# First two expert-tile steps placed in the drain of the second pass, table pieces and bias products placed elsewhere

## The chip, the cores and the metric

The kernel runs on one core of one Trainium2 chip. The metric is the device time of one execution in microseconds (us), lower is better. The engines are TensorE (PE in the rows; PEld is its weight load), VectorE (DVE), ScalarE (ACT), GpSimd (POOL) and SyncE (SP), which only issues DMAs. Every engine runs its own instruction list in order and waits on semaphores.

## What is computed

Two layers over x (16 sequences x 128 tokens x 128) and a context (16 x 120 x 128), float32:

```python
x = x + L0_xattn(layernorm(x), ctx, ctx)     # 16 heads of 8, temperature per head from score statistics
x = x + L0_ffn(layernorm(x))                 # RMS norm, router, top 2 of 8 experts, up 128->512, u * silu(gate), down 256->128
x = x + L1_xattn(layernorm(x), ctx, ctx)     # 8 heads of 128, windows of 64 keys with dilation 1, 2, 4, 8, biases bq, bk, bv, bc
x = x + L1_ffn(layernorm(x))                 # router with softmax, top 2 of 8 experts, gelu, 128->64->128
```

## The kernel before, in words

The work goes in stages. A first pass over the 16 sequences computes the scores and their statistics, then the weights are turned or multiplied on TensorE. The **second pass** (software pipeline with the `b_` functions) computes the first attention, its residual, the norm, the router's logits and the top two experts of each sequence. Then come the **tiles** of the first feed-forward layer (`ct_` functions), the **second attention** (`c_` and `d_` functions, with the norm of each sequence as its `c` tail), and the second feed-forward layer (`e_` functions).

*The second pass.* `software_pipeline` writes out one step after the other. A stage with lag k handles sequence `step - k` in that step. Sixteen sequences with lags up to 7 give 32 steps, 0 to 31, the ones from 16 on being the **drain**. On TensorE the stages of one step are, in this order: logits of sequence step-6, scores of step-1, the turn (transpose) of the normed rows of step-5, the projection of step-3, the output of step-2, and then the parts with a step number, `b_rank` and `attention_biases`. VectorE has at the end of its step the highest logits of sequence step-6 and `b_route`, which picks experts of a batch of four sequences (`pick_experts`, steps 9, 13, 17, 21), places its rows (`place_rows`, one step later, after TensorE's `rank`) and computes pieces of the tile tables (`tile_table`). GpSimd has the norm's power function (`tail_rstd`) of sequence step-3 and two scatters per step from step 11 on (`scatter`, 32 in all): each writes 128 normed rows to their places in the DRAM tensor `by_expert`, which is sorted by expert.

*The tiles.* The 4096 rows (2048 tokens, two experts each) are handled as 39 tiles of 128 rows in three phases: 9 tiles need batches 0 and 1 (scatters 0 to 15), 8 more need batch 2, and the last 22 need batch 3. Which expert a tile has and where its rows lie are data: `tile_table(k, piece)` computes the table of phase k on one partition of VectorE, in five pieces, and SyncE, ScalarE and TensorE read it into registers (`read_four`, line 457, waits for the semaphore `k_tab`). SyncE loads a tile once its table and its scatters are there (`load_tile`, wait for `k_tab` at line 465, for the scatters at 578, the DMA at 581), six tiles ahead in a ring of four, and stores the result (585). `tile_pipeline` (line 685) writes out the steps: in step n TensorE turns tile n (`ct_turn`, its matmul is line 1649), multiplies tile n-1 by the expert's up weights (`ct_up_project`, 1870) and tile n-2 by its down weights (`ct_down_project`, 1881). ScalarE copies the up weights of tile n (`ct_weights`, 826), computes the gate of tile n-1 (831) and copies the result of tile n-2 (837). VectorE copies the turned tile n (`ct_turned`, 1502), forms the product of tile n-1 (`ct_product`, 1508), and then does `ct_route`: in step 0 the copy of the bias sum, in steps 1 to 5 the pieces of table 2.

*The start of the second attention.* TensorE computes the keys of two pairs of sequences, then for sequences 0 and 1 the values, the turn of the normed rows (`c_turn`), and the scores, and then a software pipeline. VectorE combines the two expert rows of a sequence (`c_combine`, lines 1514 and 1518, inside `d_combine`), takes its statistics (1257, 1267), applies the norm (`c_norm`, 1280), and does parts of the softmax (`d_scores`, `d_weights`). GpSimd gathers the two expert rows of each sequence with two indirect DMAs (`gather`, 1065), and computes the norm's factor (`tail_rstd`, 990 and 992). `d_add_bias` (1084) adds the bias row to x.

*The bias products.* `attention_biases` (line 1746) sums bc and, over eight heads, the product of the value bias with Wc into one PSUM place: one product with `ones` and eight with a broadcast column of `bqk1`, each two matmul records in the trace. VectorE copies the sum into `bias_rows`.

## Time and profile before

| | us |
|---|---|
| median of 3 runs | 423.95 (422.66 to 426.68) |
| profiled execution, its own time | 422.5 |
| its span | 420.6 |
| busy in the span: TensorE, its weight load | 358.2 (85%), 277.4 (66%) |
| VectorE, ScalarE, GpSimd | 310.2 (74%), 279.4 (66%), 200.1 (48%) |
| mean granted TensorE clock | 0.935 of full speed |

The span is 1.9 us shorter than the execution's own time; what lies around it is launch and end. The busy time of an engine is an average over stages. The page cuts the span into 40 slices of 10.5 us and gives each engine one digit per slice (9 is 90% or more), and one for the clock that TensorE was granted:

```profile
PE   1776796655979999997699999978999999969996
PEld 0432342223766676666599999847888888756886
DVE  3599999998445999899664444378988988886752
ACT  1399999998565566642277887647888788673330
POOL 2554445554001443887779000278887783532200
PEclk9989869985889999998599999999999999997999
```

The second pass lies in slices 12 to 19 (from 120 us), the tiles in 19 to 25, the second attention in 25 to 36. The slices 18 and 19 (189 to 210 us) and 25 to 27 (263 to 294 us) hold the two borders that the change touches.

### The profile page before, as it was taken

What the parts mean: (1) busy time and instruction counts of PE and PEld (TensorE: products, weight loads), DVE (VectorE), ACT (ScalarE), POOL (GpSimd) and SP (SyncE); (2) the same over time, 40 slices, a digit from 0 to 9 for tenths busy, and PEclk for the clock granted to TensorE, in tenths of its full rate; (3) what the DMA queues carried; (4) which work ended last, traced back from release to release, by engine and by line L of the source; (5) the groups of instructions that cost most, each with busy time, mean ns of one, the idle gap of its engine ahead of it and who ended that gap; (6) DMA issues with size and microseconds to landing.
All of it is one profiled execution on the core that took longest, in us unless ns stands there. A gap on an engine that the chain in (4) does not pass through costs nothing.

```text
span 420.6 us, 12481 instructions
## 1 busy us (share of the span) xinstructions
PE 358.2 (85%) x4117; PEld 277.4 (66%) x4117; DVE 310.2 (74%) x1149; ACT 279.4 (66%) x844; POOL 200.1 (48%) x357
## 2 busy tenths in 40 slices
PE   1776796655979999997699999978999999969996
PEld 0432342223766676666599999847888888756886
DVE  3599999998445999899664444378988988886752
ACT  1399999998565566642277887647888788673330
POOL 2554445554001443887779000278887783532200
PEclk9989869985889999998599999999999999997999
DMA  5999799500010000011243332111110010000011
GB/s 109 108 302 314 199 289 291 127 2 0 2 40 6 3 6 5 29 35 34 88 124 106 95 89 83 39 39 40 27 30 25 19 27 4 2 2 1 10 43 50
DMA packets 58497, 29.88 MB, mean 71 GB/s; under 512 B 15810, under 2 KB 56004, under 8 KB 58436
## 3 DMA queue, kind: packets, MB, share of 16 engines
q1 hardware_dynamic: 53652, 23.83, 21.8%
q0 software_dynamic: 2048, 4.20, 3.5%
q10 hardware_dynamic: 2736, 1.07, 1.2%
q8 instruction: 34, 0.56, 0.6%
q14 instruction: 27, 0.22, 0.2%
HBM read 13.82 MB, written 15.27 MB: 69 GB/s over the span
## 4 chain that ended last, share of the span: by engine, by line
PE 47%; DVE 20%; issue 11%; ACT 9%; POOL 6%; DMA 2%; ACTq 2%; SPq 1%; POOLq 0%; DVEq 0%
PE psum L1870 9%; PE psum L1649 6%; ACT wa L739 5%; PE psum L1881 4%; PE psum L1895 4%; PE psum L1684 3%; DVE scored L1165 3%; DVE negmax L1152 2%; DVE work L1233 2%; PE psum L1918 2%; POOL rstd L986 2%; PE psum L2008 2%; ACTq L697 2%; PE psum L1934 2%; PE psum L1952 2%
## 5 line engine op out<-in xcount | busy, mean ns | idle before, releaser
L739 ACT ACTIVATE wa<-psum,negmax 128x120 f32<-128x120 f32 x256 | 68.3, 440 | 2.0 <-DVE negmax L1152 1.9
L1065 POOL DMA_INDIRECT c_area<-by_expert,rows_at x32 | 31.4, 980 | 50.4 <-DMA by_expert<-c_area 38.8
L1684 PE MATMUL psum<-wa 64*128 64x480 f32 x128 | 41.8, 738 | 9.6 <-issue 7.5
L954 POOL TENSOR_TENSOR wa<-kT,cst 128x960 f32<-128x960 f32 x16 | 28.6, 1791 | 37.9 <-ACT kT L720 35.0
L1165 DVE BATCH_NORM_STATS2 scored<-wa 128x6 f32<-128x240 f32 x128 | 43.2, 400 | 4.2 <-issue 4.2
L771 ACT ACTIVATE work<-psum 120x1024 f32<-120x1024 f32 x32 | 31.0, 1022 | 19.6 <-PE psum L1806 19.6
L1870 PE MATMUL psum<-c_area,work 128*128 128x128 f32 x312 | 42.8, 282 | 0.1
L1870 PEld LDWEIGHTS psum<-c_area,work 128*128 128x128 f32 x312 | 39.2, 197 | 0.3 <-issue 0.3
L1508 DVE TENSOR_TENSOR c_area<-psum,c_area 128x256 f32<-128x256 f32 x39 | 16.6, 425 | 30.8 <-ACT c_area L831 27.4
L1152 DVE TENSOR_REDUCE negmax<-psum 128x8 f32<-128x960 f32 x32 | 36.7, 1146 | 2.7 <-PE psum L1684 2.4
L1025 POOL DMA_INDIRECT by_expert<-scored,rows_at x32 | 32.2, 1006 | 8.9 <-issue 8.3
L1895 PE MATMUL psum<-ctxS,qk 128*128 128x256 f32 x128 | 29.8, 379 | 0.0
L1649 PE MATMUL psum<-cst,work 128*128 128x128 f32 x120 | 21.7, 329 | 6.3 <-issue 4.2
L852 ACT ACTIVATE work<-work,d 128x128 f32<-128x128 f32 (+1 forms) x64 | 23.1, 371 | 5.2 <-DVE d L1543 5.2
L826 ACT COPY work<-upT 128x512 f32 x39 | 24.1, 621 | 2.9 <-issue 2.9
L846 ACT COPY work<-psum 128x1024 f32<-128x1024 f32 x16 | 16.2, 1011 | 14.0 <-PE psum L1918 13.9
L1895 PEld LDWEIGHTS psum<-ctxS,qk 128*128 128x128 f32 x128 | 23.6, 193 | 2.6
L1649 PEld LDWEIGHTS psum<-cst,work 128*128 128x128 f32 x120 | 16.8, 170 | 11.8 <-issue 8.8
L1881 PE MATMUL psum<-dnT,c_area 128*128 x156 | 23.9, 276 | 0.6 <-DVE c_area L1508 0.6
L1684 PEld LDWEIGHTS psum<-wa 64*128 64x128 f32 x128 | 12.4, 222 | 17.6 <-issue 17.5
L1671 PEld LDWEIGHTS psum<-wa,w4T 128*128 128x128 f32 x32 | 5.4, 213 | 28.0 <-ACT wa L727 28.0
L881 ACT ACTIVATE work<-psum,uvec 128x256 f32<-128x256 f32 x56 | 22.0, 472 | 2.7 <-PE psum L1895 2.7
(275 smaller groups left out, 988.8 us busy)
## 6 DMA issues: line engine op xcount, KB each, us to landing
by_expert<-work SPq DMA_DIRECT2D x12, 768.0 KB, 6.6
c_area<-by_expert SPq DMA_DIRECT2D x39, 64.0 KB, 1.9
by_expert<-c_area SPq DMA_DIRECT2D x39, 64.0 KB, 1.6
x<-in_x_dram ACTq DMA_DIRECT2D x16, 64.0 KB, 3.7
work<-in_L_ffn_w_down_dram SPq DMA_DIRECT2D x1, 1024.0 KB
wa<-mscratch SPq DMA_DIRECT2D x64, 2.0 KB
out_dram<-wa SPq DMA_DIRECT2D x32, 32.0 KB, 1.6
wa<-in_ctx_dram SPq DMA_DIRECT2D x16, 60.0 KB, 3.6
```

The lines of the kernel that those rows point to most:

```text
L739: e = nc.scalar.activation(prob[:, z, head, :], psum[:, score_bank(b, half) + h // 4, (h % 4) * LK:(h % 4 + 1) * LK], ACT.Exp, bias=negmax ...
L771: nc.scalar.activation(probT[:, z, half * HALF0:(half + 1) * HALF0, :].rearrange("p h q -> p (h q)"), psum[0:LK, 2 * half:2 * half + 2, :] ...
L954: nc.gpsimd.tensor_tensor(kexp[:, z], kT[:, b, :].unsqueeze(1).to_broadcast([P, HALF0, LK]), halfscale.unsqueeze(2).to_broadcast([P, HALF0 ...
L1025: nc.gpsimd.indirect_dma_start(by_expert[:, :], bass.IndirectOffsetOnAxis(rows_at[:, i:i + 1], 0), xrow[:, BATCH * r + i % BATCH, :], None ...
L1065: nc.gpsimd.indirect_dma_start(y_rows[:, r, j, :], None, by_expert[:, :], bass.IndirectOffsetOnAxis(rows_at[:, i:i + 1], 0)).then_inc(ld_y ...
L1152: nc.vector.tensor_reduce(negmax[:, z, :].rearrange("p (a c h) -> p a c h", a=2, c=2)[:, :, half], banks(score_bank(b, half), 2)[:, :, 0:4 ...
L1165: s = nc.vector.bn_stats(bnout[:, bass.ds(b * HALF0 + h // 2, 1), :].rearrange("p a s -> p (a s)"), prob[:, z, h:h + 2, :].rearrange("p h ...
L1649: return nc.tensor.transpose(dst, src, ident[0:k, 0:k])
L1684: m = nc.tensor.matmul(psum[:, score_bank(b, half) + g, 0:4 * LK], qs[rows, z, :], kexp[rows, z, 4 * half:4 * half + 4].rearrange("p i k - ...
L1870: m = nc.tensor.matmul(psum[:, n % 2, j * P:(j + 1) * P], ct_w[:, n % 2, j * P:(j + 1) * P], ct_xT[:, n % 2, :], start=True, stop=True)
L1881: m = nc.tensor.matmul(psum[:, 4, 0:D], ct_h[:, n % 2, j * P:(j + 1) * P], w, start=(j == 0), stop=(j == DN_TILES - 1))
L1895: m = nc.tensor.matmul(psum[:, bank + i // 2, 2 * P * (i % 2):2 * P * (i % 2 + 1)], qk1[:, 4 * half + i, :], ctxS[:, 2 * p:2 * p + 2, :].r ...
```

## The change

It has four parts. (1) The pieces of table 0, in steps 15 to 18 of the second pass, are placed in steps 15 to 17. (2) Steps 0 and 1 of the tile pipeline are placed at the end of steps 20 and 21 of the second pass, on TensorE, ScalarE and VectorE (`SEAM`, `seam_tiles`; `rest_tiles` writes the remaining steps). (3) The pieces of table 1, in steps 19 to 21 of the second pass, are placed in tile steps 0 to 4, and those of table 2 in tile steps 5 to 9, not 1 to 5. (4) The bias products, in steps 18 and 19 of the second pass, are placed around the first turns of the second attention; VectorE copies their sum there, behind the norm of sequence 1 and ahead of combining sequence 2. Their place in PSUM and that of three small buffers change with it.

```diff
...
@@ -668,8 +668,9 @@
         RAMP, EARLY_PAIRS = 2, 2
         PICK_AT = {BATCH * (r + 1) - 1 + LOGITS_B: r for r in range(BATCHES)}
         TABLE_PIECES = 5
-        PIECES_AT = {15: ((0, 0),), 16: ((0, 1), (0, 2)), 17: ((0, 3),), 18: ((0, 4),),
-                     19: ((1, 0), (1, 1)), 20: ((1, 2), (1, 3)), 21: ((1, 4),)}
+        PIECES_AT = {15: ((0, 0), (0, 1)), 16: ((0, 2), (0, 3)), 17: ((0, 4),)}
+        SEAM = {NB + 4: 0, NB + 5: 1}
+        TABLE_AT = {**{n: (1, n) for n in range(TABLE_PIECES)}, **{n + TABLE_PIECES: (2, n) for n in range(TABLE_PIECES)}}
         SCATTERS = {BATCH + LOGITS_B + 1 + i: range(2 * i, 2 * i + 2) for i in range((BATCHES - 1) * BATCH)}
 
         def after(first, stage):
@@ -684,10 +685,19 @@
 
         def tile_pipeline(stages, lag=5):
 
-            for n in range(TILES + lag):
+            def step(n):
                 for late, stage in stages:
                     if 0 <= n - late < TILES or late == 0:
                         stage(n - late)
+
+            def seam(b, z):
+                if b + 7 in SEAM:
+                    step(SEAM[b + 7])
+
+            def rest():
+                for n in range(len(SEAM), TILES + lag):
+                    step(n)
+            return seam, rest
 
 
         @block.scalar
@@ -813,9 +823,6 @@
                     nc.scalar.activation(nat0[:, 3, 0:1], eps[:, 1:2], ACT.Silu)
 
             act.wait_ge(wt_dve, copied_by_dve(C_GROUPS - 1))
-            software_pipeline(act, [(6, b_logits), (1, b_softmax(0)), (1, b_softmax(1)), (5, tail_evict("b")),
-                                    (7, lambda b, z: b_halves(b + 7))], peel=NB)
-
             staged = {}
 
             def ct_weights(n):
@@ -836,7 +843,10 @@
                     act.wait_ge(st_ct[n % RING_C], 16 * (n // RING_C))
                 nc.scalar.copy(ct_y[:, n % RING_C, :], psum[:, 4, 0:D]).then_inc(ct_ye, 1)
 
-            tile_pipeline([(0, lambda n: ct_weights(n) if n < TILES else None), (1, ct_gate), (2, ct_result)], lag=2)
+            seam_tiles, rest_tiles = tile_pipeline([(0, lambda n: ct_weights(n) if n < TILES else None), (1, ct_gate), (2, ct_result)], lag=2)
+            software_pipeline(act, [(LOGITS_B, b_logits), (1, b_softmax(0)), (1, b_softmax(1)), (5, tail_evict("b")),
+                                    (7, lambda b, z: b_halves(b + 7)), (7, seam_tiles)], peel=NB)
+            rest_tiles()
 
 
             def d_vw_copy(b, z):
@@ -1418,11 +1428,6 @@
                 for piece in PIECES_AT.get(step, ()):
                     tile_table(*piece)
 
-            software_pipeline(dve, [(0, b_expand), (3, b_residual), (3, tail_stats("b", b_x1)), (4, tail_norm("b")),
-                                    (4, tail_rms), (2, b_add_bias), (2, b_recip),
-                                    (3, tail_aggr("b")), (2, b_norm), (0, b_constants), (LOGITS_B, b_highest),
-                                    (7, lambda b, z: b_route(b + 7))], peel=NB)
-
             r_done, r_after = counted(r_dve)
 
             def route_logits(half):
@@ -1487,11 +1492,8 @@
                                         own[:, at, :].unsqueeze(2).to_broadcast([P, SEQS, LQ]), ALU.mult).then_inc(e_gm, 1)
 
             def ct_route(n):
-                if n == 0:
-                    dve.wait_ge(l1_pe, L1_SUMS)
-                    nc.vector.tensor_copy(bias_rows[:, 0, :], psum[:, 5, 384:384 + D]).then_inc(l1_dve, 1)
-                elif n - 1 in range(TABLE_PIECES):
-                    tile_table(len(PHASES) - 1, n - 1)
+                if n in TABLE_AT:
+                    tile_table(*TABLE_AT[n])
                 elif n == TILES - 4:
                     expert_weights()
 
@@ -1524,7 +1526,12 @@
                 for stage in (c_combine, c_stats, c_aggr):
                     stage(b, z)
 
-            tile_pipeline([(0, lambda n: ct_turned(n) if n < TILES else None), (1, ct_product), (0, ct_route)], lag=1)
+            seam_tiles, rest_tiles = tile_pipeline([(0, lambda n: ct_turned(n) if n < TILES else None), (1, ct_product), (0, ct_route)], lag=1)
+            software_pipeline(dve, [(0, b_expand), (3, b_residual), (3, tail_stats("b", b_x1)), (4, tail_norm("b")),
+                                    (4, tail_rms), (2, b_add_bias), (2, b_recip),
+                                    (3, tail_aggr("b")), (2, b_norm), (0, b_constants), (LOGITS_B, b_highest),
+                                    (7, lambda b, z: b_route(b + 7)), (7, seam_tiles)], peel=NB)
+            rest_tiles()
 
 
             def d_keys(p, half):
@@ -1614,6 +1621,8 @@
             d_combine(1, 1)
             d_scores(0, 0)
             c_norm(1, 1)
+            dve.wait_ge(l1_pe, L1_SUMS)
+            nc.vector.tensor_copy(bias_rows[:, 0, :], psum[:, BANK_TAIL, 384:384 + D]).then_inc(l1_dve, 1)
             d_combine(2, 0)
             d_weights(0, 0)
             c_norm(2, 0)
@@ -1743,18 +1752,17 @@
             weights(range(10, N_GROUPS))
 
 
-            def attention_biases(step):
-
-                dst = psum[:, 5, 384:384 + D]
-                if step == NB + 2:
-                    pe.wait_ge(b_x1, NB)
+            def attention_biases(heads):
+
+                dst = psum[:, BANK_TAIL, 384:384 + D]
+                if heads.start == 0:
                     pe.wait_ge(l1_dve, 2)
+                    pe.wait_ge(b_lk, NB)
                     nc.tensor.matmul(dst, ones[0:1, :], bc1[:, :], start=True, stop=False)
-                heads = {NB + 2: range(3), NB + 3: range(3, H1)}.get(step, ())
                 for h in heads:
                     m = nc.tensor.matmul(dst, bqk1[:, 2, h:h + 1].to_broadcast([P, P]), wcT[:, h, :],
                                          start=False, stop=(h == H1 - 1))
-                if step == NB + 3:
+                if heads.stop == H1:
                     m.then_inc(l1_pe, 1)
 
             def tail_turn(ph):
@@ -1768,7 +1776,6 @@
                         if ph == "b":
                             pe.wait_ge(b_lk, b)
                     if ph == "c" and b == 0:
-                        pe.wait_ge(l1_dve, L1_DONE)
                         pe.wait_ge(k_rows, BATCHES)
                     if ph == "d":
                         pe.wait_ge(tails["c"]["ev"], min(NB, b + TAIL_D + RAMP - TURN_C))
@@ -1850,9 +1857,6 @@
                 if step - 1 in PICK_AT:
                     rank(PICK_AT[step - 1])
 
-            software_pipeline(pe, [(LOGITS_B, tail_logits("b", routerT)), (1, b_scores), (5, tail_turn("b")),
-                                   (3, b_project), (2, b_output), (7, lambda b, z: b_rank(b + 7)),
-                                   (7, lambda b, z: attention_biases(b + 7))], peel=NB)
             tile_expert = {}
 
             def ct_turn(n):
@@ -1882,7 +1886,10 @@
                                          start=(j == 0), stop=(j == DN_TILES - 1))
                 m.then_inc(ct_dn, 1)
 
-            tile_pipeline([(0, lambda n: ct_turn(n) if n < TILES else None), (1, ct_up_project), (2, ct_down_project)], lag=2)
+            seam_tiles, rest_tiles = tile_pipeline([(0, lambda n: ct_turn(n) if n < TILES else None), (1, ct_up_project), (2, ct_down_project)], lag=2)
+            software_pipeline(pe, [(LOGITS_B, tail_logits("b", routerT)), (1, b_scores), (5, tail_turn("b")),
+                                   (3, b_project), (2, b_output), (7, lambda b, z: b_rank(b + 7)), (7, seam_tiles)], peel=NB)
+            rest_tiles()
 
 
             def d_keys(p, half):
@@ -1946,8 +1953,7 @@
             def d_output_whole(b, z):
                 pe.wait_ge(d_aT, b + 1)
                 pe.wait_ge(d_vw, b + 1)
-                if b:
-                    pe.wait_ge(d_x, b)
+                pe.wait_ge(*((d_x, b) if b else (l1_dve, L1_DONE)))
                 for h in range(2):
                     nc.tensor.matmul(d_sum, a1T[:, z, h * P:(h + 1) * P], vw[:, (b + 1) % RING_V, h * D:(h + 1) * D], start=(h == 0), stop=False)
 
@@ -2039,7 +2045,10 @@
             for b in range(2):
                 d_values_whole(b, b)
                 d_values_tiles(b, b)
+                if b == 0:
+                    attention_biases(range(0, 3))
                 c_turn(b, b)
+                attention_biases((range(3, 5), range(5, H1))[b])
                 d_scores_whole(b, b)
                 d_scores_tiles(b, b)
             software_pipeline(pe, [(RAMP + TURN_D, d_turn), (RAMP + TAIL_D, tail_turn("d")), (RAMP + LOGITS_D, tail_logits("d", router1)),
```

## Rows read from the trace of the kernel before

**Rows 1.** chain of waits, 195 to 212: start us, length us, engine, tile, line, count
```profile
196.48 1.58 PE psum L1755 x6
...
199.07 2.13 PE psum L1755 x10
...
202.68 0.61 PE psum L1791 x2
...
204.46 0.62 DVE work L1322
```

**Rows 2.** waits of SyncE's queue, 150 to 300: total us, times, longest
```profile
SPq L465 <- DVE tile_tab L1389: 21.7, 1, 21.7
...
SPq L578 <- DMA by_expert<-scored,rows_at: 3.1, 1, 3.1
```

**Rows 3.** GpSimd in time order: start, length, line, operation, [idle before <- releaser]
```profile
197.62 0.21 POOL L980 TENSOR_TENSOR rstd<-mv,both 128x2 f32<-128x2 f32 x1
...
200.46 0.96 POOL L1025 DMA_INDIRECT by_expert<-scored,rows_at  x1 [0.30 <-issue]
```

**Rows 4.** DMA issues: tensors, queue, count, KB each, median us to landing
```profile
c_area<-by_expert SPq DMA_DIRECT2D x39, 64.0 KB, 1.9
...
by_expert<-scored,rows_at POOLq DMA_INDIRECT x32, 2.3
```

**Rows 5.** SyncE in time order: first loads of the tiles
```profile
202.91 7.04 SPq L581 DMA_DIRECT2D c_area<-by_expert  x7
```

**Rows 6.** TensorE in time order, first tile steps
```profile
205.82 0.48 PE L1649 MATMUL psum<-cst,c_area 128*128 128x128 f32 x1
...
207.31 1.93 PE L1870 MATMUL psum<-c_area,work 128*128 128x128 f32 x8
209.03 0.42 PE L1649 MATMUL psum<-cst,c_area 128*128 128x128 f32 x1
...
212.53 0.27 PE L1649 MATMUL psum<-cst,c_area 128*128 128x128 f32 x1
212.64 1.06 PE L1870 MATMUL psum<-c_area,work 128*128 128x128 f32 x8
...
213.98 0.27 PE L1649 MATMUL psum<-cst,c_area 128*128 128x128 f32 x1
...
215.76 0.30 PE L1649 MATMUL psum<-cst,c_area 128*128 128x128 f32 x1
```

**Rows 7.** windows: length; TensorE, weight loads, VectorE, ScalarE, GpSimd busy; granted clock; DMA
```profile
194.00:198.00 4.00, 3.05 (x23) 2.60 (x23) 3.68 (x23) 0.00 (x0) 3.30 (x6) 0.80 0.08 26
...
206.00:210.00 4.00, 3.23 (x15) 2.96 (x16) 1.65 (x9) 0.72 (x2) 3.09 (x4) 0.50 0.29 90
210.00:214.00 4.00, 4.00 (x37) 3.98 (x36) 2.83 (x13) 2.80 (x8) 3.09 (x4) 1.00 0.35 105
```

**Rows 8.** VectorE in time order, end of the second pass
```profile
197.11 0.18 DVE L1267 BATCH_NORM_AGGREGATE mv<-bn 128x2 f32<-128x6 f32 x1
...
198.17 0.15 DVE L1381 TENSOR_SCALAR tile_tab<-small 1x9 uint32<-1x9 f32 x1
...
199.24 0.33 DVE L1280 TENSOR_SCALAR xn<-x,mv,rstd 128x128 f32<-128x128 f32 x1
```

**Rows 9.** TensorE in time order, start of the second attention
```profile
276.65 0.33 PE L1649 MATMUL psum<-cst,c_area 128*128 128x128 f32 x1 [0.79 <-DVE c_area L1280]
...
281.04 0.33 PE L1649 MATMUL psum<-cst,c_area 128*128 128x128 f32 x1 [0.17 <-DVE c_area L1280]
...
291.20 0.66 PE L1649 MATMUL psum<-cst,work 128*128 128x128 f32 x4 [1.29 <-DVE work L1557]
```

**Rows 10.** VectorE in time order, start of the second attention
```profile
280.93 0.36 DVE L1514 SCALAR_TENSOR_TENSOR x<-c_area,ew_t,x 128x128 f32<-128x128 f32 x1
...
289.36 0.48 DVE L1280 TENSOR_SCALAR c_area<-x,work 128x128 f32<-128x128 f32 x1 [0.85 <-POOL work L992]
```

**Rows 11.** GpSimd in time order, start of the second attention
```profile
282.32 0.19 POOL L990 TENSOR_TENSOR work<-work,eps 128x1 f32<-128x1 f32 x1 [0.39 <-DVE work L1267]
```

More of the change, by code:

```diff
@@ L372, in build @@
         total_ps = keep[0:1, 192:192 + NE]
-        in_c = (area(13184, 12).rearrange("p (z s) -> p z s", z=2), area(13196, 4).rearrange("p (z s) -> p z s", z=2),
-                area(13200, 8).rearrange("p (z s) -> p z s", z=2),
+        in_c = (area(W_C, 12).rearrange("p (z s) -> p z s", z=2), area(W_C + 12, 4).rearrange("p (z s) -> p z s", z=2),
+                area(W_C + 16, 8).rearrange("p (z s) -> p z s", z=2),
                 c_area[:, 3840:4096].rearrange("p (z d) -> p z d", z=2), None)
```

## The prediction

> **What bounds the kernel now.** I read the page's slices first: TensorE is nearly full in the tiles and in the second attention, so a change at the two borders between stages pays only as far as those full stretches start earlier. Then the chain of waits over the first border. In [rows 1] the bias products of TensorE (six, then ten matmuls at the lower clock) stand on the chain, and behind them the last sequence's router logits at 202.68 and its picks on VectorE, done at 204.46 + 0.62 = 205.08. So the products do delay the last picks. But the first tile needs something else too, and for that I read the waits of SyncE's queue [rows 2]: it waited 21.7 us for the first table and then, with the table there, another 3.1 us for rows that GpSimd scatters. The table was not last. GpSimd computes the last sequence's norm at 197.62 without any idle time before it, and issues the sixteenth scatter, the last one that tile 0 needs, at 200.46 [rows 3]; this lands 2.3 us later [rows 4], at 202.8, and the first load is issued at 202.91 [rows 5]. With 1.9 us to landing [rows 4] tile 0 is there at 204.8. TensorE turns it at 205.82 [rows 6], after ranking the last batch.
>
> **Part 1: the first table one step earlier.** It was not awaited last, so nothing is won. What does it cost? VectorE is busy 3.68 of 4 us before the border [rows 7]: it is the engine that sets the pace there. Its last piece ran from 198.17 to 199.24, behind the statistics of the last sequence at 197.11 [rows 8]. Now all five pieces stand ahead of these statistics: 199.24 - 198.17 = 1.07 us later, done at 197.11 + 0.18 + 1.07 = 198.36. GpSimd, which started on them at 197.62, starts at about 198.4 instead: its sixteenth scatter, tile 0's load and its landing all come 0.8 us later, at L = 205.6. Bounds: 0 (if VectorE's gaps take the pieces) and 1.1 us. I take 0.8, since 3.68 of 4 us leaves no gap for it.
>
> **Part 2: two tile steps in the drain.** On TensorE the turn of tile 0 now stands ahead of the last sequence's logits, and it waits for the load until L. Before, the logits ran at 202.68. Queued behind the wait are the logits, then the picks on VectorE, the ranks and the last batch's row places. From L: turn and copy to SBUF as before; the logits slip in beside that copy; the second turn at L + 0.8; the up products of tile 0 at L + 1.0, 1.93 us at the lower clock [rows 6], until L + 2.8 as TensorE issues. The picks take, from logits to end, 205.08 - 202.68 = 2.4 us [rows 1], and VectorE has a table piece of about 0.6 us in front of them: they end at about L + 2.9, after the up products. Then the rank, 205.82 - 205.08 = 0.7 us [rows 1, 6], and the turn of tile 2 at L + 3.7 = 209.3. Before it was at 209.03 [rows 6]. So the first border gives nothing: +0.3 us. The two steps are inside the drain by their place in the program, but they run at the time at which they ran before, since the data arrives then. Bounds: with L at 204.8, and the rank hidden behind the up products, -1.3 us; with one more tile step at the lower clock, +1.7 us. I take +0.3, which the rows give directly.
>
> What leaves this stretch is the bias work: 18 matmuls. The copy of the sum by VectorE also leaves; it was beside other work. ScalarE's copies of the weights and its first gate are small and find the engine idle. SyncE's order of loads and stores is the same; tile 9's load now waits for a table that ends with tile step 4, about when the load's ring is free anyway (its turn comes four steps later).
>
> **Part 3: both later tables among the tiles.** A tile step is 1.45 us (213.98 - 212.53), and one in which VectorE has a long table piece was 215.76 - 213.98 = 1.78 us, 0.33 more [rows 6]. Before, five pieces lay in tile steps; now ten do, two of them in the drain. The new ones are of eight tiles, not 22, hence shorter; only the last, with its bookkeeping for the next table, is as long. One such loss and a bit: +0.4 us, bounds 0 and 3 x 0.33 = 1.0.
>
> **Part 4: the bias products in the second attention.** At the higher clock eight matmuls start over 1.06 - 0.27 us, 0.11 each [rows 6]. The first group (8 matmuls, 0.9 us) stands before the turn at 276.65, where TensorE idled 0.79 [rows 9]: 0.1 us at most. The second (4, 0.4 us) runs while ScalarE copies that turn. The third (6 matmuls) follows the turn at 281.04 [rows 9]; TensorE itself would wait there for ScalarE, so on TensorE it is hidden. But VectorE now waits for the sum, in order, right before it combines sequence 2. Queued behind this wait: that combination (before at 280.93, without idle time) [rows 10], its statistics, the first softmax weights. The sum is there at 281.15 + 6 x 0.11 + 0.27 = 282.1; with the copy VectorE goes on at 282.3. That is 1.3 us late. Is that hidden? GpSimd waited 0.39 us for exactly these statistics at 282.32 [rows 11], and from there it is full: gathers of sequences 4 and 5, the norm of sequence 3, for which VectorE waits 0.85 us at 289.36 [rows 10], and with that TensorE at 291.20 (1.29 us idle) [rows 9], where its full stretch begins. Each link is the late one, so the 1.3 us go through. Bounds: 0 (if the sum is ready before VectorE comes to it) and 1.8 us (six matmuls at 0.21 each, the pace of the lower clock).
>
> **Sum.** 0.3 + 0.4 + 1.3 = +2.0 us, on the profiled execution's 422.5 us: 424.5. The three timed runs have a median of 423.95 and spread over 4 us, so the profiled one is at the low end; the four values together have a middle of 423.3. I predict the median as 423.3 + 2.0 = 425.3 us.
>
> **Rivals.**
> (A) *The freed TensorE wins.* VectorE's earlier pieces fall into gaps, tile 0 lands at 204.8 as before, its up products start near 205.9, not 207.31, and the wait at the second attention is hidden: -1.4 + 0.4 + 0 = -1.0, 422.3 by the middle above. For: the products are on the chain [rows 1]. Against: VectorE has no gaps [rows 7], and GpSimd sets the load.
> (B) *TensorE's clock stays low longer; slower.* The granted clock was 0.50 (1.2 GHz) from 206 to 210, and 1.00 (2.4 GHz) in the next 4 us [rows 7], after some 3 us of dense products that followed a sparse stretch. Now TensorE has no bias products and waits about 4 us for tile 0, then alternates with VectorE. If the rise comes later, each tile step at the lower clock has 12 matmuls and a turn at 0.21 instead of 0.11 us, about 1.35 us more. It decides from two steps on: 2.0 + 2.7 = +4.7, 428.0. Against: from L on the density is nearly what it was from 205.8 on.
> The Trainium skill (TensorE: Matmul & The Clock Gate, "What's actually happening") says the same as a rule: the throttled state is the default, and sustained activity releases it. By that rule, thinning out TensorE's work ahead of the tiles speaks against this change.
> (C) *Only the second border is harmless:* the sum is awaited in time that VectorE would lose anyway. +0.7, 424.0. Against: VectorE showed no idle time at 280.93.
>
> **How the numbers follow.** Forecast 0.55, A 0.14, B 0.12, C 0.14, something unseen 0.05. 1% of this kernel, 4.2 us, is what a measurement can tell from no change. The forecast, A and C lie within it. Slower by over 1%: most of B, and a little of the forecast with the spread of the runs: 0.14. Faster by over 1%: a slice of A and of the unseen, 0.07. The range: 421.5 (A with its spread) to 428.6 (B, and the upper bounds of parts 2 and 4); its own width for the forecast alone is 423.3 to 427.2.
>
> **What would show it.** SyncE's wait for the scattered rows longer than 3.1 us, and the wait for the table shorter by the same reordering; the first load issued near 203.7; the last logits right behind the turn of tile 0, near 206, instead of 202.68; the turn of tile 2 within 0.5 us of 209.03; one or two tile steps above 1.45 us more than before; VectorE idle about 1 us before the copy of the bias sum, released by TensorE; the first idle-free turn of the attention 2 us after 291.20. The prediction is wrong if the load of tile 0 is issued before 203, if tile 2 is turned before 208, or if GpSimd does not wait longer for the statistics of sequence 2.

## The result and the profile after

The changed kernel takes 428.39 us (median of 8 runs, 425.57 to 430.48), the kernel before beside it 423.47 us (8 runs, 422.46 to 426.68): a ratio of 1.0087, 95% interval 1.0051 to 1.0123. Run a second time it took 428.23 us against 424.01 (medians of 12 and 29 runs), ratio 1.0078 (1.0036 to 1.0120). Each ratio is an estimate over the runs and not the quotient of the two medians, which lie 4.9 and 4.2 us apart here; it leaves out runs in a slower state, over 1.5% above the fastest of their kernel (one each of e2_late_copy and e7_bias_late, three of e12_all_three). So the changed kernel is slower by 0.8 to 0.9%, some 3.5 us, by the ratios, and by 1.0 to 1.2% by the medians; the forecast was 425.3 us, +2.0. Its lowest time is 3.25 us above the lowest of the kernel before in that second comparison (425.10 against 421.85), its highest 2.80 us (430.64 against 427.84): the whole spread has moved by about 3 us.

I call the first profiled execution of the changed kernel "after" (429.23 us, span 427.3) and the second one "the second profile" (425.76 us, span 423.9). They are 3.4 us apart, with one program; that is used below.

**The first border.** SyncE's queue in the changed kernel, 150 to 300 us: total wait, times, longest; it answers to [rows 2].

```profile
SPq L465 <- DVE tile_tab L1399: 20.0, 2, 19.5
...
SPq L578 <- DMA by_expert<-scored,rows_at: 6.5, 1, 6.5
```

The wait for the table is 2.2 us shorter than before (19.5 against 21.7), the wait for the scattered rows 3.4 longer (6.5 against 3.1): the earlier table buys nothing. GpSimd in time order (start, length, line, operation, idle before and its releaser), to be set beside [rows 3]:

```profile
199.16 0.19 POOL L990 TENSOR_TENSOR rstd<-mv,both 128x2 f32<-128x2 f32 x1 [0.63 <-DVE mv L1277]
...
202.02 0.96 POOL L1035 DMA_INDIRECT by_expert<-scored,rows_at  x1 [0.30 <-issue]
```

The last norm had no idle time before it; now GpSimd waits 0.63 us for VectorE's statistics, which stand behind the table. The sixteenth scatter is at 202.02, not 200.46, and the first load at 204.48, not 202.91. TensorE in time order, beside [rows 1, 6]:

```profile
206.48 0.48 PE L1658 MATMUL psum<-cst,c_area 128*128 128x128 f32 x1 [4.89 <-DMA c_area<-by_expert]
206.75 0.44 PE L1798 MATMUL psum<-routerT,xnT 128*128 128x8 f32 x2
207.44 0.45 PE L1658 MATMUL psum<-cst,c_area 128*128 128x128 f32 x1 [0.25 <-DVE c_area L1504]
207.67 1.94 PE L1874 MATMUL psum<-c_area,work 128*128 128x128 f32 x8
...
210.11 0.48 PE L1658 MATMUL psum<-cst,c_area 128*128 128x128 f32 x1
210.38 1.92 PE L1874 MATMUL psum<-c_area,work 128*128 128x128 f32 x8
212.09 1.06 PE L1885 MATMUL psum<-dnT,c_area 128*128 x4
212.94 0.42 PE L1658 MATMUL psum<-cst,c_area 128*128 128x128 f32 x1
```

TensorE stands 4.89 us before the turn of tile 0, and the last logits, at 202.68 before, are now behind it at 206.75. Tile 0's up products start at 207.67, 0.36 us later than before. Then comes what the sum did not hold: the second up products take 1.92 us, not 1.44, and the down products 1.06, not 0.61. The next two rows are windows (busy times of the five units, granted clock, DMA share and GB/s), first of "after", then of the second profile; they answer to [rows 7].

```profile
210.00:214.00 4.00, 4.00 (x21) 3.97 (x21) 2.52 (x13) 1.71 (x5) 3.09 (x4) 0.51 0.22 68
```

```profile
210.00:214.00 4.00, 4.00 (x36) 4.00 (x36) 2.96 (x16) 2.20 (x6) 2.97 (x4) 0.98 0.33 98
```

Before, the granted clock was 1.00 (2.4 GHz) in this window. In "after" it stayed at 1.2 GHz nearly to its end, in the second profile it did not. From 206 to 210 TensorE had been busy 3.27 of 4 us in "after", 3.75 in the second profile and 3.23 in the kernel before, where the clock rose early too; so the busy time in that window does not tell the two cases apart.

**The tables.** VectorE and then GpSimd in "after":

```profile
225.56 1.97 DVE L1399 TENSOR_SCALAR tile_tab<-small 1x22 uint32<-1x22 f32 x1
227.45 0.27 DVE L1504 COPY c_area<-psum 128x128 f32<-128x128 f32 x1
```

```profile
226.24 1.26 POOL L1050 TENSOR_TENSOR w_lo<-ew,w_hi 128x512 fp32r<-128x512 f32 x1
```

A write of 22 numbers takes 1.97 us, ends at 227.53, 0.03 us after GpSimd's subtraction (227.50), and TensorE waits 1.67 us for the copy behind it; this tile step is 3.37 us long, and 1.76 before. In the second profile the same write lies earlier:

```profile
223.72 0.17 DVE L1399 TENSOR_SCALAR tile_tab<-small 1x22 uint32<-1x22 f32 x1
...
225.94 0.42 DVE L1510 TENSOR_TENSOR c_area<-psum,c_area 128x256 f32<-128x256 f32 x1 [0.95 <-ACT c_area L838]
```

**The second border.** VectorE, GpSimd and TensorE in "after", to be set beside [rows 9, 10, 11]:

```profile
286.89 0.29 DVE L1625 COPY small<-psum 128x128 f32<-128x128 f32 x1 [1.09 <-PE psum L1763]
287.10 0.34 DVE L1516 SCALAR_TENSOR_TENSOR x<-c_area,ew_t,x 128x128 f32<-128x128 f32 x1
```

```profile
288.47 0.19 POOL L1000 TENSOR_TENSOR work<-work,eps 128x1 f32<-128x1 f32 x1 [2.06 <-DVE work L1277]
```

```profile
297.39 0.66 PE L1658 MATMUL psum<-cst,work 128*128 128x128 f32 x4 [1.56 <-DVE work L1564]
```

VectorE waits 1.09 us for the sum of the bias products and then copies it; GpSimd's wait grows from 0.39 to 2.06 us, and the turn at which the full stretch begins goes from 291.20 to 297.39.

**The loss by stretch.** Five points can be read in every trace: the first reciprocal of the second pass on VectorE (129.42 before), the turns of tile 4 (212.53) and tile 20 (236.44), the turn of [rows 9] at 291.20, and the end of the span (420.6). The stretches between them, each less that of the kernel before, in us:

| profiled execution | start | border 1 | tables | border 2 | rest | span |
|---|---|---|---|---|---|---|
| after | +0.44 | +1.87 | +2.25 | +1.63 | +0.51 | +6.7 |
| the second profile | -0.05 | +0.36 | +0.61 | +2.10 | +0.28 | +3.3 |
| e1_bias_in_drain | +3.95 | +1.26 | +0.64 | +0.01 | -0.06 | +5.8 |
| e2_late_copy | +0.12 | +1.88 | +2.26 | +0.22 | +0.52 | +5.0 |
| e3_no_seam | +0.10 | -0.19 | +0.81 | +1.61 | +0.57 | +2.9 |
| e4_bias_only | +0.82 | +0.68 | -0.14 | +2.17 | +0.57 | +4.1 |
| e10_pool_waits | -0.32 | +0.30 | +0.61 | +2.46 | +0.05 | +3.1 |
| e11_fill | +4.25 | +3.01 | +2.32 | +1.63 | +0.49 | +11.7 |
| e12_all_three | +0.45 | +2.69 | +0.40 | +0.23 | +0.43 | +4.2 |

Three things in it belong to no kernel but to the execution. (1) The start is near 0 or near +4 (+0.82 in e4). Windows of the kernel before and of e11_fill, 127 to 134 us, in code that no kernel here changes:

```profile
127.00:134.00 7.00, 6.76 (x158) 4.62 (x154) 3.36 (x8) 3.88 (x4) 0.59 (x2) 1.00 0.02 5
```

```profile
127.00:134.00 7.00, 6.47 (x80) 4.21 (x84) 0.33 (x1) 2.32 (x3) 0.30 (x1) 0.53 0.02 4
```

The same 7 us hold half the matmul records at half the clock (1.2 GHz); e1_bias_in_drain shows 0.51 there, e4 0.76. (2) At the first border the granted clock falls between 195.6 and 197.6 in each trace with a start near 0 (in e12 it is low once more before that, from 190.8 to 194.2), and is back near 210 (before, the second profile, e3, e10) or between 212.7 and 214.7 (after, e2, e4, e12). (3) The table write meets GpSimd's subtraction in after, e2 and e11, and in none with the early clock. So a comparison of two profiles needs partners of the same kind. The second profile is such a partner of the profile before, and its +3.3 us is what the ratios of the timed runs show too.

### The profile page after: what moved, and what is told of

Its sections match the earlier page's. It is cut to its first block, busy times and chain, and to the rows that moved or that the text cites. A ratio compares the mean times of both kernels' runs of the same rounds, so it can differ in the third digit from the quotient of the medians.

```text
span 427.3 us, 12481 instructions
## 1 busy us (share of the span) xinstructions
PE 358.6 (84%) x4117; PEld 277.6 (65%) x4117; DVE 311.7 (73%) x1149; ACT 279.5 (65%) x844; POOL 200.1 (47%) x357
## 3 DMA queue, kind: packets, MB, share of 16 engines
q10 hardware_dynamic: 2736, 1.07, 1.2%
## 4 chain that ended last, share of the span: by engine, by line
PE 47%; DVE 20%; issue 11%; ACT 9%; POOL 6%; DMA 2%; ACTq 2%; SPq 1%; POOLq 0%; DVEq 0%
PE psum L1874 8%; PE psum L1658 6%; PE psum L1902 6%; ACT wa L749 5%; PE psum L1885 4%; PE psum L1693 3%; DVE scored L1175 3%; PE psum L1925 2%; DVE negmax L1162 2%; DVE work L1243 2%; POOL rstd L996 2%; ACTq L707 2%; PE psum L2014 2%; PE psum L1941 2%; PE psum L1958 1%
## 5 line engine op out<-in xcount | busy, mean ns | idle before, releaser
L1874 PE MATMUL psum<-c_area,work 128*128 128x128 f32 x312 | 43.7, 285 | 0.0
L1874 PEld LDWEIGHTS psum<-c_area,work 128*128 128x128 f32 x312 | 40.1, 201 | 0.0
L1658 PE MATMUL psum<-cst,work 128*128 128x128 f32 x120 | 21.7, 329 | 7.8 <-issue 4.2
```

Source lines behind the costliest of these rows:

```text
L1658: return nc.tensor.transpose(dst, src, ident[0:k, 0:k])
L1874: m = nc.tensor.matmul(psum[:, n % 2, j * P:(j + 1) * P], ct_w[:, n % 2, j * P:(j + 1) * P], ct_xT[:, n % 2, :], start=True, stop=True)
```

## The experiments

The comparison of the first four was with 35 runs of the kernel before, median 424.24 us, that of the next four with 29 runs, median 424.01 us.

**e1_bias_in_drain**: part 4 undone, the rest of the change kept.

```diff
-                if b == 0:
-                    attention_biases(range(0, 3))
                 c_turn(b, b)
-                attention_biases((range(3, 5), range(5, H1))[b])
...
+                (7, lambda b, z: attention_biases({NB + 2: range(3), NB + 3: range(3, H1)}[b + 7])
+                    if b + 7 in (NB + 2, NB + 3) else None),
...
```

> The changed kernel with part 4 undone: the bias products stand again in steps 18 and 19 of the second pass, VectorE copies their sum in tile step 2. Theory (costs are: scatters later 0.7 us, TensorE's clock low longer 1.2, table pieces among tiles 0.5, bias sum awaited by VectorE in the second attention 1.6): the products run in time in which TensorE idles anyway before tile 0 arrives, so the turn of tile 0 stays near 206.5 and the 1.6 us at the second attention go: about 1.6 us below the changed kernel, ratio to before about 1.006; GpSimd's wait for the statistics of sequence 2 is 0.4 us again. Rival (the bias products cost the drain as much as they cost the attention): same time as the changed kernel, ratio 1.010, and the turn of tile 0 comes later than 206.5.

425.80 us, ratio 1.0036 (1.0002 to 1.0071). The second border costs +0.01 instead of +1.63 and +2.10: that loss is part 4's alone. More than half of the timed loss is gone with it (1.0087 and 1.0078 to 1.0036, though the intervals still touch).

**e2_late_copy**: as changed, but VectorE copies the sum behind the combination and the statistics of sequence 2.

```diff
             c_norm(1, 1)
-            dve.wait_ge(l1_pe, L1_SUMS)
-            nc.vector.tensor_copy(bias_rows[:, 0, :], ...)
             d_combine(2, 0)
+            dve.wait_ge(l1_pe, L1_SUMS)
+            nc.vector.tensor_copy(bias_rows[:, 0, :], ...)
```

> The changed kernel with VectorE's wait for the bias sum and its copy moved behind the combination of sequence 2. Theory (VectorE's wait in order is what costs): VectorE idles under 0.2 us there, GpSimd gets the statistics of sequence 2 about 1.3 us earlier and the first idle-free turn of the attention comes 1.3 us earlier relative to the last tile; ratio to before about 1.006. Rival (the products on TensorE themselves, or the gathers, set that stretch): less than 0.4 us are won.

426.52 us, ratio 1.0044 (1.0006 to 1.0082). VectorE in time order:

```profile
285.40 0.35 DVE L1516 SCALAR_TENSOR_TENSOR x<-c_area,ew_t,x 128x128 f32<-128x128 f32 x1
...
286.61 0.27 DVE L1626 COPY small<-psum 128x128 f32<-128x128 f32 x1
```

The combination starts with no idle time, the copy with none either, 1.2 us later: by then the sum is there. The second border costs +0.22. The 18 matmuls on TensorE are thus nearly free, and the place of one wait in VectorE's order was the price. Border 1 and the tables repeat those of "after" within 0.01 us, the held write of 1.96 us with them (tile step 3.36 us).

**e3_no_seam**: as changed, but no tile step in the drain.

```diff
-        SEAM = {NB + 4: 0, NB + 5: 1}
+        SEAM = {}
```

> The changed kernel with part 2 undone: no tile step in the drain, tables and bias products as changed. Theory (the wait for tile 0 ahead of the last logits holds up picks, ranks and with them dense work on TensorE): the last logits run near 202, the turn of tile 2 comes 0.5 to 1 us earlier than in the changed kernel, the clock rises 1 to 4 us earlier, and the kernel is 1 to 2 us faster than the changed one, ratio to before about 1.006. Rival (the two steps in the drain do help): slower than the changed kernel by 0.5 us or more, ratio above 1.010.

427.10 us, ratio 1.0067 (1.0032 to 1.0102). TensorE in time order:

```profile
201.76 0.60 PE L1798 MATMUL psum<-routerT,xnT 128*128 128x8 f32 x2 [0.46 <-ACT xnT L807]
...
206.03 0.48 PE L1658 MATMUL psum<-cst,c_area 128*128 128x128 f32 x1 [1.05 <-DMA c_area<-by_expert]
```

Without the bias products the last logits start 0.92 us earlier than in [rows 1], and the last ranking too; but now the first tile's load, 1.3 us later than before because of part 1, is awaited last. The border gives 0.19 us back where the seam, in an execution with the same clock, costs 0.36. The timed interval overlaps that of the changed kernel, so the gain from leaving the seam out is read from the traces alone.

**e4_bias_only**: only part 4; tables and tile steps where they were.

> The kernel before with part 4 alone. Theory: the drain loses up to 0.9 us (the turn of tile 0 can come at 204.9, when its rows land, instead of 205.8), the second attention costs 1.6 us more: 0.7 to 1.6 us slower than before, ratio 1.002 to 1.004. Rival (freeing TensorE in the drain is worth the 4 us that the products took on the chain): faster than before, ratio 0.996 or less.

425.18 us, ratio 1.0029 (0.9992 to 1.0066). The second border costs +2.17, the tables nothing. Its first border costs 0.68 with the late clock: the window from 210 to 214 has 0.66. So the late clock also comes in a kernel without the seam.

**after_again**: the changed kernel.

> The changed kernel itself, beside the next three. If the lost time is the change's own and not one chip's: a ratio of 1.0087 again, within 0.0035, the granted clock 0.5 until after the up products of tile 1, and the last piece of table 2 at 1.97 us, not 0.17, behind an operation of GpSimd. If the long last piece was a late fetch of instructions that depends on the chip or on the run: it is 0.17 here.

428.23 us, ratio 1.0078 (1.0036 to 1.0120), as told above. The loss is there again. But against the expectation the profile shows the early clock and a write of 0.17 us: so a loss of some 3 us is there without them, and the late clock and the held write come on top in some executions.

**e10_pool_waits**: GpSimd's subtraction waits until the last table is written (the added wait stands behind GpSimd's power operation; the expectation speaks as if it stood ahead of it).

```diff
+            pool.wait_ge(k_tab, len(PHASES))
             pool.wait_ge(rounded, 2)
```

> The changed kernel, but GpSimd begins its powers of the expert weights only when the last table is written (one wait more on GpSimd). Theory, that VectorE's write of the last table entries is held until GpSimd's subtraction ends: the write takes 0.17 us, tile step 10 takes about 1.5 us, not 3.4, and the time is 1.7 us less than that of the changed kernel on this chip (ratio 0.9960 to it), unless GpSimd's later start is missed by the gathers. Rival, a late instruction fetch on VectorE: the write still takes about 2 us and the time does not move.

427.34 us, ratio 1.0067 (1.0026 to 1.0107), 0.9 us below the changed kernel, which these intervals do not tell from nothing. Its profile has the early clock, and there the write (223.38, 0.17 us) is far ahead of the subtraction (225.49) anyway; nothing was to be taken away, and this run doesn't decide. **e11_fill** tells more.

**e11_fill**: 18 turns of the unit matrix on TensorE in step 20, where it waits for tile 0.

```diff
+            def keep_clock(step):
+                for _ in range({NB + 4: 18}.get(step, 0)):
+                    turn(psum[:, 3, 0:P], ident, P)
...
+                                   (7, lambda b, z: keep_clock(b + 7)), (7, seam_tiles)], peel=NB)
```

> The changed kernel, with 18 turns of the unit matrix more on TensorE in step 20 of the second pass, where it waits for the first tile; their results are not read. Theory B, that the low clock of the first tile steps costs one to two steps' worth: the granted clock rises before the first up products, these take about 1.1 us, not 1.9, and the third tile is turned 1 to 2 us earlier relative to the first load; the time is 1 to 2 us less than the changed kernel's. Rival, that data and VectorE set these steps: the clock rises, and the third tile's turn stays within 0.4 us.

429.73 us, ratio 1.0123 (1.0060 to 1.0185): not faster, and the border costs +3.01. TensorE in time order, then two windows:

```profile
205.81 3.84 PE L1658 MATMUL psum<-cst 128*128 128x128 f32 x18
210.95 0.33 PE L1658 MATMUL psum<-cst,c_area 128*128 128x128 f32 x1 [1.30 <-DMA c_area<-by_expert]
...
211.89 1.27 PE L1878 MATMUL psum<-c_area,work 128*128 128x128 f32 x8
```

```profile
209.00:212.00 3.00, 1.36 (x10) 1.06 (x9) 0.65 (x3) 0.55 (x2) 2.39 (x3) 0.95 0.49 152
213.00:219.00 6.00, 5.44 (x34) 5.18 (x34) 3.27 (x16) 2.06 (x5) 4.58 (x5) 0.50 0.28 87
```

The clock did rise with the fillers, the first up products took 1.27 us, not 1.93. But TensorE then idled for the load, busy 1.36 of 3 us, and the clock was 0.50 again from 213 to 219, through the dense steps. Fillers that end before the work begins raised the clock here for the idle time. Of the +3.01 us, 1.74 lie ahead of the first load and 1.27 between it and the turn of tile 4, where "after" has 1.13 and 0.74. The third turn comes 5.5 us after the first load, as in the changed kernel (5.6 and 5.5 us): that is the rival's case. The profiled execution is the slowest of the six timed ones. The Trainium skill, "TensorE: Matmul & The Clock Gate", section "What's actually happening", ties the clock to TensorE's recent activity; both edges here agree in kind (the same fillers in e12, below, were followed by no rise), while the two profiles of the changed kernel, alike in activity and 3.7 us apart in the rise, show that this case's rows don't suffice to forecast the edge. The held write is in this trace on another line:

```profile
230.20 1.69 DVE L1391 TENSOR_SCALAR tile_tab<-small 1x22 uint32<-1x22 f32 x1
```

```profile
230.60 1.26 POOL L1050 TENSOR_TENSOR w_lo<-ew,w_hi 128x512 fp32r<-128x512 f32 x1
```

It ends at 231.89, again 0.03 us after the subtraction's 231.86. A late fetch of VectorE's code would belong to a place in its code; this stall goes with the subtraction. No run moved the subtraction away from a write that it would have met.

**e12_all_three**: the changed kernel with e2's late copy, e10's wait and e11's fillers.

> The changed kernel with all three: GpSimd's powers after the last table, the turns of the unit matrix in step 20, and the copy of the bias sum behind the combination of sequence 2. If the three terms add (1.7, 1 to 2, 1.3 us): 4 to 5 us less than the changed kernel, and so 0 to 1.5 us less than the kernel before, ratio 0.9965 to 1.0. If each is taken back by the next late one (the last picks, the gathers, the norm of sequence 3): 1 to 2 us less than the changed kernel, and still slower than the kernel before.

428.34 us, ratio 1.0065 (1.0015 to 1.0115): it is no better than the changed kernel by any bound that counts. The second border is cheap again (+0.22 in e2, +0.23 here): this term comes back. The write takes 0.17 us in spite of the late clock, but not by the added wait: the write ends at 226.51, GpSimd's power runs until 227.12, and the subtraction follows it (227.10) without idle time. The first border costs +2.69, with the rise only at 214.7. This time no rise followed the fillers; TensorE in time order, then a window in them and one behind them:

```profile
202.36 4.05 PE L1659 MATMUL psum<-cst 128*128 128x128 f32 x18
```

```profile
204.00:205.00 1.00, 1.00 (x7) 1.00 (x6) 0.00 (x0) 0.00 (x0) 0.74 (x1) 0.50 0.20 66
...
209.00:210.00 1.00, 1.00 (x6) 1.00 (x6) 0.93 (x5) 0.00 (x0) 0.70 (x2) 0.50 0.52 152
```

Nor is the +2.69 the fillers' cost. Tile 0's load is at 205.45, 0.97 us later than in "after"; GpSimd had waited 1.64 us for statistics until 195.73 (0.62 in "after"), right behind the stretch from 190.8 to 194.2 in which the granted clock was low, and well ahead of the fillers. From the turn of tile 0 to that of tile 4 it is 8.35 us, as in "after" (8.36). One of the three terms comes back, the other two were not put to the test that they were meant for.

**On one other chip** four kernels ran beside a kernel before of 450.27 us (median of 31 runs), so their ratios are not to be set beside those above: e5_table0_early (part 1 alone, in the kernel before), e6_fill and e9_pool_waits (the same kernels as e11 and e10), and e7_bias_late (part 4 alone, with the late copy).

> The kernel before with part 1 alone: the pieces of table 0 in steps 15 to 17. Theory (the scatters set tile 0's load, and VectorE has no gap): relative to the start of the second pass the sixteenth scatter and the first load come 0.8 to 1.2 us later, while in this kernel the turn of tile 0 still waits for the last picks' ranks, which gain nothing either; 0 to 1.2 us slower, ratio 1.000 to 1.003. Rival (the first table was what the tiles waited for): the first load is issued earlier and the kernel is faster, ratio below 0.998.

450.99 us, ratio 1.0013 (0.9984 to 1.0042).

> The changed kernel with 18 turns of the identity into an unused PSUM bank, on TensorE, in the 4.9 us in which it waits for tile 0 (step 20). They compute nothing that is used. Theory (about 1.2 us, and the low clock of the first tile steps with it, are the price of the idle wait): the granted clock rises before or at tile step 1, the first up products take 0.9 to 1.1 us and not 1.94, tile 4 is turned 2 us earlier relative to tile 0, and the kernel is about 2 us faster than the changed one, ratio about 1.004. Rival (the wait for tile 0 and VectorE's chain set these steps, whatever the clock): less than 0.5 us are won, ratio 1.008.

447.88 us, ratio 0.9948 (0.9917 to 0.9978).

> The kernel before with the bias products in the second attention, and VectorE's copy of their sum behind the combination of sequence 2. Theory (the wait in order is what part 4 costs, the products themselves 0.3 us; the drain gains up to 0.9 us): between 0.6 us faster and 0.5 us slower than before, ratio 0.998 to 1.001; about 1 us faster than part 4 alone. Rival (the gathers set the start of the attention in any case, or the sparse drain keeps TensorE's clock low longer and takes the gain back): no faster than part 4 alone, ratio 1.003 or more.

447.96 us, ratio 0.9949 (0.9917 to 0.9980).

> The changed kernel with one wait more on GpSimd: the subtraction of 128x512 elements that follows its power operation (line 1050) starts only when table 2 is done. Theory (VectorE's last write of table 2, 1.97 us instead of 0.17, was held by that GpSimd subtraction, which ended 0.03 us before it): the write takes 0.2 us, tile step 10 takes about 1.5 us and not 3.37, the kernel is about 1.7 us faster than the changed one, ratio about 1.005. Rival (VectorE's instructions were fetched late there): the write still takes about 2 us and the time is that of the changed kernel, ratio 1.009.

446.77 us, ratio 0.9918 (0.9884 to 0.9952). ScalarE of e7_bias_late, in time order:

```profile
228.43 0.38 ACT L839 ACTIVATE c_area<-psum 128x256 f32<-128x256 f32 x1 [18.60 <-remote]
```

ScalarE stands 18.60 us before its gate of an early tile, for something that the trace only calls remote, which it names no instruction for; in e5 it is 19.43 us, in e6 and e9 it comes in shorter pieces (at most 4.64 us), and no trace of the other chips has it. The first border of these four traces is 11 to 25 us longer than in the profile before, so what moves such a stall outweighs all else in the ratios there. They say nothing on part 1 or on the fillers, and whether the changed kernel as it is would be slower on that chip too was not tried.

## Why the prediction was right, and where its sum was not

Right in direction and, step by step, in the mechanism: slower, by waits at the places that it names. The size was too small. The median of 428.39 us lies inside the stated range by 0.2 us only (421.5 to 428.6), above the forecast's own width (up to 427.2) and nearest to rival B's 428.0: that the range held it is owed to what was added for B and for the upper bounds, and so in part to luck. Of the signs, the load (204.02 and 204.48, forecast 203.7), the last logits (206.16 and 206.75, forecast near 206) and GpSimd's longer wait (1.73 and 2.06 us, 0.39 before) came; the third turn was to be within 0.5 us of 209.03 and was 0.49 and 1.08 late; the first idle-free turn of the attention came 3.0 and 6.2 us late, not 2. None of the three signs of being wrong came. By its steps, against the second profile, whose clock at the first border is that of the profile before (VectorE, SyncE, TensorE, and VectorE and TensorE at the second border):

```profile
198.45 0.18 DVE L1277 BATCH_NORM_AGGREGATE mv<-bn 128x2 f32<-128x6 f32 x1
...
204.02 6.46 SPq L581 DMA_DIRECT2D c_area<-by_expert  x7
...
209.52 0.48 PE L1658 MATMUL psum<-cst,c_area 128*128 128x128 f32 x1
...
283.74 0.29 DVE L1625 COPY small<-psum 128x128 f32<-128x128 f32 x1 [1.09 <-PE psum L1763]
...
294.22 0.66 PE L1658 MATMUL psum<-cst,work 128*128 128x128 f32 x4 [1.54 <-DVE work L1564]
```

- **Part 1.** The table was indeed not awaited last. Predicted: tile 0's load 0.8 us later, bounds 0 and 1.1. Measured 1.1 us (202.91 to 204.02), the upper bound: VectorE gave none of the table work back. That work grew from 1.07 to 1.22 us, with two operations at 0.42 and 0.34 us that took 0.16 and 0.15 before, and the statistics came 1.34 us later (197.11 to 198.45); GpSimd took up the rest: it started 0.33 us after their end before, and starts 0.09 us after it now. Part 1 ran alone only on the chip with the stalls, so this is read from the traces of all four parts together.
- **Part 2.** Predicted +0.3 us, measured +0.36, by the steps given: tile 0 turned at 205.89, its up products at 207.08 (1.2 us later, forecast 1.0), the picks done at 208.78, the third turn behind them. The gain of rival A is visible only in e3_no_seam (-0.19), and it is eaten by part 1's late load.
- **Part 3.** Predicted +0.4, bounds 0 and 1.0; measured +0.61.
- **Part 4.** Predicted +1.3 from VectorE's wait and copy; in "after" 1.09 + 0.2 us, in the second profile the combination of sequence 2 comes 3.01 us late where the one before it was 1.66 late, that is 1.35. Every link named passed it on. This is the term of the sum that was most too small: the border cost 2.10 us, and 1.63 in "after". What was missing is 0.3 us of the first product group, before the first turn ("0.1 us at most" was wrong: 281.52 against 276.65, 4.87 us late, where 4.56 had been brought along), and in the second profile 0.77 us by which the first gather landed later (VectorE's idle before the combination 1.71 us, 0.94 before). From the gather's issue to that combination it is 4.80 us there and 5.18 in e10, against 4.03 before, 3.98 in "after" and 3.89 in e3: so it seems to belong to the execution and not to the change. Why it landed later is open.
- **The sum.** +2.0 against +3.3: the border and the tables were off by 0.1 and 0.2, the second border by 0.8, and 0.3 lies behind it. The timed ratios, 3.7 and 3.3 us, agree with that; the medians, 4.9 and 4.2 us apart, hold the late clock too, as far as the two profiles tell.
- **Rival B** happened, in "after": the late clock costs about 1.5 us at the first border (1.87 against 0.36), near the 1.35 per step of the prediction, and one step only. It brings the tile steps later, GpSimd's subtraction by 0.5 us only (226.24 against 225.74), and so the two meet: the held write, 1.6 us more. Together they are 3.1 of the 3.4 us between the two profiles. But e4 has the late clock without the seam, and the timed spread of before (6 us) is as wide as that of after. Over 3 us above the lowest of their set lie 10 of the 20 timed runs of the changed kernel and 20 of the 72 of the kernel before: this points to a change that makes the longer executions more frequent, and is too little to show it.
- **Rival C**, a harmless second border, is false as put, and true for e2_late_copy: there it costs 0.2 us.

Beside a kernel before of 424 us no kernel tried beats it. The nearest are part 4 alone (1.0029) and the change without part 4 (1.0036). Part 4 alone with the late copy would be the next to try there; it ran only on the other chip, where it was 0.5% faster than the kernel before, but so were two variants of the changed kernel (0.5 and 0.8%), with the stalls told above.

## What to carry to other kernels

A part of a prologue is worth moving earlier only if the thing awaited last moves too: here the table was early already, and pushing it ahead of the statistics delayed the scatters that were last. When work goes under another engine's cover, its products are often free and its consumer's place is not: put the wait and the copy at the last point of the consumer's order that its reader allows (1.4 us here). And before a difference of 1% between two profiles is explained, profile one kernel twice.

## What was not expected of the hardware

**VectorE held by GpSimd.** Three times (after, e2, e11) a VectorE operation of 22 elements from SBUF to SBUF, 0.17 us otherwise, took 1.69 to 1.97 us and ended 0.03 us after GpSimd's 128x512 subtraction. It had started 0.40 to 0.68 us before the start that the trace gives for the subtraction; a write that started 0.76 us before it (e12) was not held. In the second profile VectorE's product of 0.42 us at 225.94, which reads PSUM, ran within the subtraction (225.74 to 227.00) at its usual length. GpSimd's power before it (2.94 us from 223.32 in "after") let a like write through in 0.16 us at 224.94. On the other chip the subtraction met another operation of VectorE, a comparison of two rows from SBUF that takes 0.27 to 0.33 us elsewhere; in e6_fill, VectorE and then GpSimd:

```profile
234.18 1.78 DVE L1366 TENSOR_TENSOR small<-counts,work 1x128 f32<-1x128 f32 x1
```

```profile
234.56 1.25 POOL L1050 TENSOR_TENSOR w_lo<-ew,w_hi 128x512 fp32r<-128x512 f32 x1
```

It ends 0.15 us after the subtraction; in e5_table0_early, where it started 0.78 us after the subtraction did, it took 0.62 us and ended 0.14 us after it; there VectorE was plainly the later of the two. The Trainium skill, "SBUF — State Buffer", section "Who interferes with whom", says that a tensor-scalar operation from SBUF can take a port pair shared with GpSimd, that the later of the two is then blocked for the whole instruction, and that an operation with at most one SBUF input outside these modes is not. The held write and the product that reads PSUM agree with that; that VectorE, whose start is shown first, was the one to wait does not, unless the starts that the trace gives for GpSimd are late. In e12 the added wait did not keep them apart, since GpSimd did not idle there; no run here takes the hold away by design, and that the port is the cause is argued, not shown.

**One program, two clocks.** The granted clock in the unchanged stretch from 127 to 134 us was 1.00 in the kernel before and 0.53 in e11_fill, whose second pass starts 4.25 us later; at the first border it rose near 210 or some 2.7 to 4.7 us later. In e12 TensorE was busy without idle time from 202.1 to 206.4, and but for 0.25 us from 207.3 on, at a granted clock of 0.50 all the time, and the rise came at 214.7. What tips it was not found.
